# A new order of stages in the queues of four engines, in the recurrent layer of a four-layer kernel

## The reference, cut to what matters

```python
def _bitlinear(x, w, nw):            # nw: weights of the norm
    xn = x * rsqrt(mean(x*x) + 1e-08) * nw
    scale = 127.0 / max(max(abs(xn)), 1e-05)          # per token
    xq = clip(round(xn * scale), -128, 127) / scale
    return xq @ ternary(w).T
params = ...                          # six rows per sequence, from c
mx = _layernorm(x) * (1 + sc_msa) + s_msa
i, f, g = _bitlinear(mx, wi, ni), sigmoid(_bitlinear(mx, wf, nf)), _bitlinear(mx, wg, ng)
h_t = f_t * h_(t-1) + silu(i)_t * (1 - f)_t           # along the tokens
o = _rmsnorm(h, gn, 1e-05) * silu(g)
x = x + g_msa * _bitlinear(o, wo, no_)
y, u = split(_bitlinear(_layernorm(x) * (1 + sc_mlp) + s_mlp, wm1, nm1))   # 2 x 512
x = x + g_mlp * _bitlinear(silu(y) * u, wm2, nm2)     # 512 -> 128
```

## Time and profile before

| | |
|---|---|
| median of 3 runs | 441.14 us (439.18 to 441.73) |
| the profiled execution | 440.3 us |
| its span, first to last instruction | 438.6 us |
| mean granted TensorE clock | 0.938 of full speed |
| busy: PE, DVE, ACT, POOL | 348.1, 307.8, 243.1, 127.2 us |

### The profile page before, as it was taken

The page is one execution under the profiler, slowest core; times in us unless marked ns, Lnnn a source line. Parts: engine busy times, 40 slices in busy tenths (PEclk is TensorE's granted clock), DMA queues, the critical chain, the costliest instruction groups (busy, mean ns, idle before and its releaser), DMA issues.

```text
span 438.6 us, 6414 instructions
## 1 busy us (share of the span) xinstructions
PE 348.1 (79%) x2234; PEld 165.3 (38%) x2247; DVE 307.8 (70%) x793; ACT 243.1 (55%) x431; POOL 127.2 (29%) x223
## 2 busy tenths in 40 slices
PE   0026968678978689899999988899887899889787
PEld 0013833343433454222222222476553444344255
DVE  0678688787967878979999962355678787776331
ACT  2277728656155631357777788635351466656652
POOL 0012202062326350643323104021430244444430
PEclk9999596998978899759999999999999899999899
DMA  7970006200000024300000000000046000000001
GB/s 236 419 296 0 2 0 143 49 1 0 1 1 0 0 56 129 107 3 1 3 3 2 3 1 2 0 1 0 0 114 176 5 3 3 2 3 5 2 0 49
DMA packets 12157, 20.01 MB, mean 46 GB/s; under 512 B 2614, under 2 KB 11066, under 8 KB 11450
## 3 DMA queue, kind: packets, MB, share of 16 engines
q1 hardware_dynamic: 12124, 19.59, 14.2%
HBM read 12.51 MB, written 0.52 MB: 30 GB/s over the span
## 4 chain that ended last, share of the span: by engine, by line
PE 40%; DVE 34%; ACT 9%; POOL 6%; issue 6%; DMA 2%; SPq 2%; DVEq 0%; POOLq 0%; ACTq 0%
DVE nm L978 12%; PE ps L1559 9%; PE ps L1545 6%; PE ps L1632 3%; POOL rstd L352 3%; PE pe L1584 3%; DVE st L540 2%; PE pe L1466 2%; PE ps L1288 2%; PE ps L1518 2%; ACT scr L1103 2%; SPq L330 2%; DMA big<-in_wa 1%; ACT tern L1040 1%; ACT junk L1095 1%
## 5 line engine op out<-in xcount | busy, mean ns | idle before, releaser
L978 DVE TENSOR_REDUCE nm<-ps 128x1 f32<-128x512 f32 (+2 forms) x224 | 132.1, 646 | 20.7 <-PE ps L1545 19.4
L1238 ACT ACTIVATE scr<-pe 128x1024 f32<-128x1024 f32 (+3 forms) x128 | 106.3, 866 | 58.9 <-PE pe L1584 58.0
L1545 PE MATMUL ps<-big 64*128 64x512 bf16 (+3 forms) x256 | 66.3, 360 | 5.4 <-DVE nm L978 2.0
L1559 PE MATMUL ps<-scr 128*32 128x512 f32 (+3 forms) x512 | 59.7, 538 | 6.3 <-ACT scr L1205 4.8
L352 POOL TENSOR_TENSOR rstd<-var,half 128x4 f32<-128x4 f32 x26 | 28.7, 1104 | 98.6 <-DVE var L549 73.3
L1584 PE MATMUL pe<-big 64*128 64x512 bf16 (+3 forms) x256 | 44.1, 359 | 3.0 <-ACT scr L1238 2.0
L1545 PEld LDWEIGHTS ps<-big 64*128 64x128 bf16 x256 | 19.5, 96 | 49.7 <-DVE nm L978 40.3
L451 POOL TENSOR_SCALAR_AFFINE_SELECT scr<-scr 128x256 f32<-128x256 f32 x64 | 25.8, 410 | 37.2 <-ACT scr L1238 35.8
L1288 PE MATMUL ps<-tern,cmask 128*128 128x512 bf16 x90 | 26.5, 435 | 0.4 <-issue 0.2
L1584 PEld LDWEIGHTS pe<-big 64*128 64x128 bf16 x256 | 12.9, 95 | 31.9 <-ACT scr L1238 17.8
L1253 ACT ACTIVATE scr<-pe,col 128x512 f32<-128x512 f32 x24 | 16.3, 688 | 15.1 <-PE pe L1466 15.1
(11 more groups left out here) (235 smaller groups left out, 614.8 us busy)
## 6 DMA issues: line engine op xcount, KB each, us to landing
big<-tern SPq DMA_DIRECT2D x48, 128.0 KB, 2.4
big<-in_wa SPq DMA_DIRECT2D x1, 2304.0 KB, 12.3
w<-in_w SPq DMA_DIRECT2D x2, 1152.0 KB, 19.2
big<-in_wa SPq DMA_DIRECT2D x1, 1344.0 KB, 5.9
big<-in_w SPq DMA_DIRECT2D x1, 1024.0 KB, 14.1
w<-in_w SPq DMA_DIRECT2D x1, 896.0 KB, 19.8
rowg<-in_rowg SPq DMA_DIRECT2D x1, 832.0 KB, 18.1
row<-in_row SPq DMA_DIRECT2D x1, 640.0 KB, 14.3
```

Of the source, the lines that this page charges most:

```text
L978: v.tensor_reduce(dst, src[:, 0:w * len(hs)].rearrange("p (h w) -> p h w", w=w), AX.X, ALU.max, negate=True).then_inc(sem(f"a{a}_max"), 1)
L1238: s_.activation(P[:, kt % 2, 2 * p:2 * p + 2, q0:S], E[(e - 1) % 2][:, :, q0:S], ACT.Exp, scale=SCALE).then_inc(sem(f"a{a}_p"), 1)
L1545: last = t_.matmul(dst[:, k * wd:(k + 1) * wd], stack_of(a, 0, b, HG * g + h, qt * 128, (qt + 1) * 128), stack_of(a, 1, b, HG * g + h, 0, ...
L1559: last = t_.matmul(bank[6][32 * h:32 * h + 32, q0:S], V[b][:, kt, HG * g + h, :], P[:, kt % 2, h, q0:S], start=(kt == 0), stop=(kt == TB - 1),
```

## The change

Every loop over batches and tiles of the recurrent layer is written out as single calls, and these are put into a new order in the queues of VectorE, ScalarE, TensorE and GpSimd (GpSimd's order comes out as before). Four roundings (`ints` of the output projection and of the MLP's input) move from VectorE to ScalarE, as `turned_ints`. The load of the Silu table moves from before the output projection's quantisation to behind the first squares of the MLP. Fill matmuls are counted and placed anew. Joined to it: more fills at the starts of the attentions, `unit_out` one exponential earlier in the causal attention, and two semaphores merged into others.

```diff
@@ VectorE (main order)
+            a_product(0, 2)
+            a_product(0, 0)
+            mean_square(0, "ss_a", ssq[:, 0, bt(0)], D, 1e-8, "ms_a")
+            a_product(0, 1)
             a_factors(0)
-            for m in range(3):
-                a_product(1, m)
-                a_ints(0, m)
+            a_product(1, 1)
+            mean_square(1, "ss_a", ssq[:, 0, bt(1)], D, 1e-8, "ms_a")
+            a_product(1, 2)
+            a_product(1, 0)
             a_factors(1)
+            a_ints(0, 0)
+            a_ints(0, 1)
+            a_ints(0, 2)
+            a_ints(1, 0)
             a_dequantised(0)
-            for m in range(3):
-                a_ints(1, m)
+            a_ints(1, 1)
+            a_ints(1, 2)
             scan_input(0)
...
             scan(1)
+            u_mean_square(0)
             gated_scan(1)
-            u_mean_square(0)
             mean_square(1, "ss_o", ssq[:, 1, bt(1)], D, 1e-5, "ms_o")
-            o_product(1)
             o_factors(0)
             u_mean_square(1)
-            ints(0, 0, "qm_oT", 1, 0, "qT_o")
+            o_product(1)
             o_factors(1)
             o_residual(0)
-            ints(1, 0, "qm_oT", 2, 4, "qT_o")
+            o_residual(1)
             modulated(0, "ln_b_root", 3 * D, "mx_b")
-            o_residual(1)
             mean_square(0, "ss_b", ssq[:, 0, bt(0)], D, 1e-8, "ms_b")
             b_product(0)
+            b_factors(0)
             modulated(1, "ln_b_root", 3 * D, "mx_b")
-            b_factors(0)
             mean_square(1, "ss_b", ssq[:, 0, bt(1)], D, 1e-8, "ms_b")
             b_product(1)
-            ints(0, 0, "qm_bT", 1, 2, "qT_b")
             b_factors(1)
             hidden(0)
             hidden(1)
-            ints(1, 0, "qm_bT", 2, 6, "qT_b")
...
+            hidden(2)
+            hidden_max(0)
+            hidden_max(1)
+            hidden(3)
+            hidden_max(2)
+            hidden(4)
+            hidden_max(3)
             h_mean_square(0)
-            hidden(TB + 1)
+            hidden(5)
+            hidden_max(4)
             h_factors(0)
...
@@ ScalarE
+            def turned_ints(b, wait, bk, done):
+                act.wait_ge(sem(wait), b + 1)
+                s_.activation(qT[:, 0, b], bank[bk], ACT.Identity, bias=magic[:, 1:2]).then_inc(sem(done), 1)
...
+            gates_a(0)
+            scan_copy(0)
+            gates_a(1)
+            scan_squares(0)
+            scan_copy(1)
+            scan_squares(1)
+            quantise(0, "fac_o", 1, vq[1], 0, vq[1], "qm_o")
+            turned_ints(0, "qm_oT", 0, "qT_o")
+            quantise(1, "fac_o", 2, vq[1], 0, vq[1], "qm_o")
+            turned_ints(1, "qm_oT", 4, "qT_o")
+            mlp_squares(0)
+            table(ACT.Silu)
+            quantise(0, "fac_b", 1, xn, 0, xn, "qm_b")
+            mlp_squares(1)
+            turned_ints(0, "qm_bT", 2, "qT_b")
             gate(0)
+            gate(1)
+            quantise(1, "fac_b", 2, xn, 0, xn, "qm_b")
+            gate(2)
+            gate(3)
+            turned_ints(1, "qm_bT", 6, "qT_b")
+            hidden_squares(0)
+            hidden_squares(1)
+            gate(4)
+            hidden_squares(2)
+            hidden_squares(3)
+            gate(5)
...
@@ TensorE
-            keep_warm(2, 56)
...
+            keep_warm(5, 11, True)
+            turn_a(0, 0)
+            keep_warm(5, 2, True)
+            turn_a(0, 1)
+            keep_warm(5, 6, True)
+            turn_a(0, 2)
+            turn_a(1, 0)
+            products_a(0)
...
+            turn_scan(1)
+            keep_warm(2, 15, True)
+            turn_o(0)
+            keep_warm(2, 2, True)
+            product_o(0)
+            keep_warm(2, 4, True)
+            turn_o(1)
+            keep_warm(2, 2, True)
+            product_o(1)
+            keep_warm(2, 41, True)
+            turn_b(0)
+            keep_warm(6, 4, True)
+            hidden_product(0)
+            hidden_product(1)
+            keep_warm(6, 4, True)
+            hidden_product(2)
+            hidden_product(3)
+            turn_b(1)
...
             attention_turn(0, 0)
-            hidden_out(B * TB - 2)
+            hidden_out(6)
+            keep_warm(2, 1, True)
             attention_products(0, 0, (0,))
-            hidden_out(B * TB - 1)
             attention_products(0, 0, (1,))
             attention_values(0, 0)
+            hidden_out(7)
@@ the attentions
-                        keep_warm(0, 8, False)
+                        keep_warm(0, 12, False)
...
-                        if x[0] == "max" and x[2] >= START_FILL[a]:
+                        if x[0] == "max" and (x[1] or x[2] >= START_FILL[a]):
                             keep_warm(4, 1, False)
...
-                                if kt == 1 and p == int(causal) and u >= 1:
+                                if kt == 1 and p == 0 and u >= 1:
                                     unit_out(u - 1)
```

More of the change, by code:

```diff
@@ L387, in gated_weights, with gated_by_norm @@
                 pool.wait_ge(sem("wg"), n + 1)
-            for b in range(B):
+            def gated_by_norm(b):
                 pool.wait_ge(sem("sig_g"), b + 1)
@@ L393, in _, with hidden_weighted @@
                                         ALU.mult).then_inc(sem("gg"), 1)
-            for b in range(B):
-                root("ms_o", b)
-                root("ms_u", b)
-            for stage in ("ln_b", "ms_b"):
-                for b in range(B):
-                    root(stage, b)
-            for t in range(B * TB):
+            def hidden_weighted(t):
                 pool.wait_ge(sem("hu"), t + 1)
@@ L518, in _ @@
             link(last)
[L519 removed]
+            dve.sem_inc(sem("params_rows"), 1)
             def modulation(l):
@@ L1125, in _, with scan_copy, scan_squares, mlp_squares @@
                 s_.activation(sg[2][:, s], vq[2][:, s], ACT.Sigmoid).then_inc(sem("sig_g"), 1)
[L1126 to L1127 removed]
+            def scan_copy(b):
                 act.wait_ge(sem("ifT"), b + 1)
                 s_.copy(hT[:, b], bank[4 * b + 1]).then_inc(sem("fT"), 1)
[L1130 to L1134 removed]
+            def scan_squares(b):
+                row_squares(b, "u_a", lambda b, i, t: bank[4 * b + 3][:, i * D:(i + 1) * D], 1, "ss_o")
+                row_squares(b, "u_a", lambda b, i, t: vq[0][:, t], 2, "ss_u")
+            def mlp_squares(b):
                 row_squares(b, "mx_b", lambda b, i, t: mx[:, t], 0, "ss_b")
[L1136 to L1137 removed]
             def gate(t):
@@ L1363, in _, with turn_o, product_o, turn_b @@
                 last.then_inc(sem("o_tok"), 1)
-            keep_warm(0, 22)
-            for b in range(B):
+            def turn_o(b):
                 pe.wait_ge(sem("qm_o"), b + 1)
                 turn(4 * b, vq[1], b, "qm_oT")
-                keep_warm(2, 2)
+            def product_o(b):
                 pe.wait_ge(sem("qT_o"), b + 1)
                 product(4 * b + 1, 0, b, WO).then_inc(sem("y_o"), 1)
-                if b == 0:
-                    keep_warm(2, 8)
+            def turn_b(b):
+                pe.wait_ge(sem("qm_b"), b + 1)
+                turn((2, 6)[b], xn, b, "qm_bT")
             def hidden_product(t):
@@ new lines, in _ @@
+            hidden_product(4)
+            keep_warm(7, 2, True)
+            hidden_product(5)
+            keep_warm(7, 1, True)
+            hidden_product(6)
+            keep_warm(7, 4, True)
+            hidden_product(7)
+            keep_warm(7, 6, True)
+            turned_hidden(0)
+            turned_hidden(1)
+            hidden_out(0)
+            turned_hidden(2)
+            hidden_out(1)
+            turned_hidden(3)
+            hidden_out(2)
+            keep_warm(7, 3, True)
```

181 lines of the change are left out of this document (92 added, 89 removed).

## The result

The changed kernel takes 430.81 us (median of 6 runs, 426.87 to 436.68); the kernel before, run beside it, 440.37 us (6 runs, 439.18 to 444.94). The ratio is 0.9737, 95% interval 0.9693 to 0.9781: 2.6% faster; the medians differ by 9.6 us. The ratios of this document leave out every run that took over 1.5% longer than the fastest of the same kernel (here the two near 436.6 us, two of six in e3, three of six in e1 and in e10, seven of eleven in e8), so each is to be read beside its range.

The account below looks back on a forecast made before the run. The recurrent layer was taken as bound by latency, two batches passing one chain of small stages in written order. From the profiled 440.3 us, -8.5 + 1.0 - 1.2 - 0.3 = -9.0 gave 431.3 us, range 427 to 437.5.

Parts of the forecast that it names:

- The lead: Recurrent layer: new queue order brings the first attention product 8.9 us earlier, of which 8.5 is handed on.
- the walk: Recurrent layer's new queues followed with old durations at 2.4 GHz: `gate(0)` at 120.65, first attention product at 149.5 us.
- its own sign: Hidden layer's first gate: prediction wrong if `gate(0)` is not 7 to 9 us earlier.
- The clock in the layer (+1.0): TensorE between 117 and 149 us: partial half clock adds 1.0, from a possible 0 to 6 us.
- another of the prediction's own signs: TensorE's queue in the layer: prediction wrong if fills end after the input of the turn behind them.
- the six us of TensorE on the path: TensorE work on the path between 117 and 149 us; half clock there would add 0 to 6 us.
- The first attention's start (-1.2): Eight more fills keep TensorE's clock: -1.2 taken, at most 2.7 gained, 3.6 lost if the clock falls.
- The second attention (-0.3, with `unit_out` 0): Four more fills at its start gain 0.3, at most 0.6 us; `unit_out` one exponential earlier moves nothing.
- Full clock: Rival, chance 0.12: no clock fall in the layer and the whole 2.7 in the first attention: 428.5 us.
- Half clock through the hidden layer: Rival, chance 0.15: too few fills in the hidden layer, price 3 to 6 instead of 1: 433.5 to 438.5 us.
- the lead that isn't there: Rival, chance 0.05: an unseen input holds some layer stage in place: 438.5 to 442 us.
- the slow fills: Rival, chance 0.06: half-clock fills hold `turn_b(0)` 6.5 us, plus 6 behind and 3.6 in the first attention: 448 us.

Follow-up runs that it names:

- e3: Changed kernel with `unit_out` back at its old place in the causal attention; 429.0 us, ratio 0.9747.
- e1: Changed kernel with attention fills and `unit_out` as before, merged semaphores kept; 435.28 us, ratio 0.982.
- e10: Changed kernel with the old fills again at the causal (second) attention's start only; median 434.92 us, ratio 0.9788.
- e8: Changed kernel without the 11 fills ahead of `turn_a(0,0)`; 437.65 us over 11 runs, ratio 0.9739 from its four shortest.
- e7: Changed kernel without the 41 fills ahead of `turn_b(0)`; 431.68 us, ratio 0.981.
- e13: Changed kernel without its new fills at both attentions' starts, `unit_out` still one exponential early; median 432.89 us, ratio 0.9831.
- e4: Changed kernel with the four roundings back on VectorE; 428.9 us, ratio 0.9746.
- e12: Changed kernel with old fills at the causal attention's start and two more fills in TensorE's gaps in the first attention; median 432.08 us, ratio 0.9797.
- e9: Changed kernel with `modulated(1)` and batch 1's squares moved ahead, so both MLP inputs precede the first wait; 435.49 us, ratio 0.9894.
- e11: Changed kernel with two more fills where TensorE stands still among the first attention's maxima; median 427.86 us, ratio 0.9718.

## Why the prediction came out

The forecast, 431.3 us, lies 0.5 above the median; as a change, -9.8 against 441.14 and -9.6 measured. Its mechanism, the lead by the order handed on whole, was right. That it came so near is luck: no run lies within 1.9 us of the median, which is the middle of 428.9 and 432.72. In the profiled pair the forecast of -9.0 stands against -11.4, and the terms were off by 0.3 (lead with clock, and the start's +0.69), 1.15 (first attention) and 0.96 (second).

**The lead.** Forecast -8.5, then +1.0 for the clock. From the start of the token stages the walk gives 149.5 - 64.77 = 84.73 us to the first product. Eight of the experiments with the new order measured 84.47 to 84.62 (e1, e3, e7, e8, e10 to e13), a lead of 9.0 to 9.2 (up to 1.3 of it perhaps the old order's clock, as said above); the changed kernel's own profile has 85.17. To `o_residual(0)` the walk has 37.93 against 38.03 to 38.15 in these; to `gate(0)` 55.88, measured 56.45 to 56.57, 0.6 late, of which about 0.4 stand at `fac_b(0)` already; to the end it makes up 0.8. By its own sign the prediction was to be wrong if `gate(0)` was not 7 to 9 us earlier: it was 6.21 earlier, through these 0.6, the start and the clock of the next paragraph, and the layer's end made up for part of it.

**The clock in the layer (+1.0): charged at the wrong place.** Behind `gate(0)` it fell in the changed kernel (136 to 142 us, 0.72), but this cost nothing: e13 ran 136 to 144 at 1.00 and took 28.02 us from `gate(0)` to the product, the changed kernel 28.09. What the changed kernel's profile lost against those eight, 0.7 us, lies for 0.6 ahead of `scan(0)` (23.50 behind the start, against 22.92 in e13), where the prediction charged nothing. There its clock was 0.51 from 63 to 73 us, in e13 0.68 (e4, whose clock fell as early, has the same late `scan(0)`). The fills ahead of `turn_a` then end later than the input of the turn behind them, which is another of the prediction's own signs, and VectorE stands for it; the changed kernel first, then e13:

```profile
79.07 1.46 PE L1340 MATMUL pe<-tern,cmask 128*128 128x512 bf16 x6
80.37 0.60 PE L1375 MATMUL ps<-ident,scr 128*128 128x128 f32 x4
...
81.01 0.69 DVE L720 TENSOR_SCALAR qT<-ps 128x512 bf16<-128x512 f32 x1 [0.90 <-PE ps L1375]
```

```profile
80.21 0.69 DVE L720 TENSOR_SCALAR qT<-ps 128x512 bf16<-128x512 f32 x1 [0.21 <-PE ps L1375]
```

The start itself came 0.69 us later than before; it lies between 63.67 and 65.50 in all the profiles, and what moves it was not looked into. Around `gate(0)` a half clock cost nothing while it ended by the rounding (e1, e3, e7, e12, e13), and 0.5 to 1.3 us, by estimate, where it lay on the first hidden product (e9, e4). So the six us of TensorE on the path were an upper bound, mostly covered by the waits behind `mlp_squares(1)` and VectorE, but not free.

**The first attention's start (-1.2): mis-sized, and it is two values.** -2.35 when the clock holds (17.64 to 17.34 and 91.00 to 88.95), close to the bound of 2.7 that VectorE's work gave; +4.0 to +4.6 when it falls all the same (21.6 to 22.2), where the bound was +3.6. I took a middle. Between the two ends lie some 6 to 7 us, the largest part of the 9.8 from 426.87 to 436.68; that the two runs near 436.6 are at the upper end is likely but not shown, since neither has a trace.

**The second attention (-0.3, with `unit_out` 0).** -1.26 in the profiled pair: +0.85 for the fills, -2.11 behind. Of that `unit_out` is 0.4 to 0.5 (e1 and e3 against the changed kernel) and the rest the clock, which fell in the kernel before in 340 to 348 and 408 to 416 (0.79 in each) and did not fall in e1. The prediction counted neither the price of the fills nor the second fall. It gave the four fills behind the last values no worth; e10 and e12, which lack them and the four among the maxima, are 4 us slower there than the changed kernel, e1 and e13 are not, and no run parts the two groups.

**The roundings.** 0.69 us on ScalarE, as estimated between two rows, and VectorE's own takes 0.69 too. The Trainium skill's table in Trainium Architecture — The Big Picture, section "The five engines, in one table", has VectorE up to about three times as fast per element in simple arithmetic; for this rounding from PSUM to bf16 the traces show no such factor.

**The rivals.** Full clock (428.5, chance 0.12): its time is what e11 reaches (426.99 to 428.79) and two of six runs of the changed kernel, though not by its condition, since the clock did fall in the layer (near 65, 96 and 137 us in e11's profile). Half clock through the hidden layer and the lead that isn't there were not seen. Of the slow fills the part in the first attention was (forecast 3.6, measured 4.0 to 4.6 in e8 to e10), the part in the layer was not, and e7 shows that the 41 fills, on which it rested, could go without a loss up to the first attention product.

## What to carry to other kernels

In a layer bound by latency, walk each queue and look for the stage whose input comes late while work of the other batch stands behind it; here some 8 to 9 us lay in such places and none in a shorter operation. Fills between instructions that matter can lose the clock all the same, and are then paid at half speed: in this kernel those with gaps of 0.34 and 0.45 us left among them lost it in three of eight profiles. So look at what idle time remains, not only at the number of fills. Where runs of one kernel differ by 2%, look in the profiles for the stretch in which the clock differs before anything is credited to an edit: e4's loss ahead of `gate(0)` is such a case.

## What the runs showed of the hardware

The same instructions of the first attention, within 0.05 us of each other from 164 to 171 us, went on at 2.4 GHz in e11 and at 1.2 GHz in e10; the only difference in TensorE's queue up to there was two fills of 0.22 us. This pair alone proves no cause: the changed kernel, whose queue up to there is that of e10, went on at 2.4 GHz. In the layer the clock fell again and again at the same stages, near 63 to 67 us in all twelve profiles with the new order, near 97 and again at 137 to 142 in eight of them, near 118 to 121 in six. What a fall cost there depended on what waited for TensorE: nothing that can be seen behind 138 us in the changed kernel, 0.6 us ahead of `scan(0)`, and up to 1.3 us by estimate at e4's first hidden product.

A rounding of 128x512 from PSUM to bf16 took 0.69 us on ScalarE and 0.69 us on VectorE.
